# A third score slot, a buffer of its own for the attention output, eight gelu tiles in place of twelve, and new order lists

## The reference

```
x = x + attn(layernorm(x))     # 16 heads of 8; q = elu(q)+1, k = elu(k)+1
                               # weights = (rope(q) . rope(k)) / (q . k); out = weights @ v @ w_out + b_out
x = x + ffn(layernorm(x))      # router: softmax over 8 experts, the best 2, weights renormalized
                               # h = gelu(x @ W1[e] + b1[e]), y = h @ W2[e] + b2[e], all 8 experts;
                               # out = sum of y * combine + shared expert; F = 512
x = x + mamba(layernorm(x))    # in-projection, 4-tap conv, silu, dt = softplus(...)
                               # h = exp(dt*A)*h + dt*B*x, y = h . C, 16 states, 256 channels; norm, gate, out
x = x + ffn(layernorm(x))
```

## Time and profile before

| | us |
|---|---|
| median of 3 runs | 4017.41 (4011.95 to 4021.06) |
| the profiled execution | 4019.45 |
| its span | 4017.3 |
| PE busy | 3458.3 (86%) |
| ScalarE busy | 3227.9 (80%) |
| VectorE busy | 2936.5 (73%) |
| GpSimd busy | 1559.3 (39%) |
| DMA, mean share | 44.8% on the one hardware queue |

### The profile page before, as it was taken

How to read it: one execution, slowest core, us unless ns; L and a number is a source line. 1 busy time by engine, 2 the same in 40 slices (tenths; PEclk the granted TensorE clock), 3 DMA queues, 4 the chain that set the end, 5 groups by cost and what they waited for, 6 DMA issues and landing times.

```text
span 4017.3 us, 38974 instructions
## 1 busy us (share of the span) xinstructions
PE 3458.3 (86%) x11446; PEld 1464.2 (36%) x11446; DVE 2936.5 (73%) x3513; ACT 3227.9 (80%) x4037; POOL 1559.3 (39%) x758
## 2 busy tenths in 40 slices
PE   3786698989899898989989898989989898898847
PEld 1141233434333343433334343433334343344424
DVE  2427768788696868879696877869697886959592
ACT  3677688888888888988989888888988888886653
POOL 1112235435253544425253543524354442415261
PEclk9586799999999999999999999999999999998978
DMA  4142445544444545444544444545454444434432
GB/s 147 45 136 61 128 144 150 156 141 141 149 145 147 152 136 162 144 143 140 155 146 145 147 145 151 147 140 149 145 155 139 150 140 150 145 108 139 131 129 71
DMA packets 214852, 552.05 MB, mean 137 GB/s; under 512 B 25105, under 2 KB 96626, under 8 KB 214642
## 3 DMA queue, kind: packets, MB, share of 16 engines
q1 hardware_dynamic: 214642, 549.57, 44.8%
HBM read 488.65 MB, written 63.18 MB: 137 GB/s over the span
## 4 chain that ended last, share of the span: by engine, by line
PE 47%; DVE 19%; ACT 16%; issue 13%; POOL 4%; DMA 1%; SPq 1%; ACTq 0%; POOLq 0%; DVEq 0%
PE bank L782 15%; PE bank L734 5%; PE bank L771 5%; ACT rPool L884 4%; ACT L1022 4%; DVE ws L1220 4%; PE bank L712 4%; PE bank L673 4%; DVE rPool L1108 4%; PE bank L773 3%; PE bank L772 3%; PE bank L707 3%; DVE ws L1227 3%; ACT hF L884 3%; DVE ws L1216 2%
## 5 line engine op out<-in xcount | busy, mean ns | idle before, releaser
L782 PE MATMUL bank<-hF,wst 128*128 128x512 f32 x2304 | 1212.1, 643 | 68.3 <-DVE tmp L1178 62.6
L1108 DVE TENSOR_TENSOR rPool<-bank,rPool 128x512 f32<-128x512 f32 x1024 | 700.2, 684 | 461.1 <-PE bank L712 431.8
L884 ACT ACTIVATE hF<-bank,cols 128x512 f32<-128x512 f32 x1152 | 771.2, 687 | 249.7 <-PE bank L773 240.5
L1328 POOL TENSOR_TENSOR yM<-yM,ws 128x1024 f32<-128x1024 f32 x240 | 742.6, 3094 | 471.9 <-DVE ws L1227 461.1
L1313 POOL TENSOR_TENSOR acc<-acc,tmp 128x512 f32<-128x512 f32 x240 | 442.6, 1844 | 1123.1 <-DVE tmp L1178 1116.8
L884 ACT ACTIVATE rPool<-bank 128x512 f32<-128x512 f32 x1040 | 574.9, 594 | 271.2 <-PE bank L707 217.9
L1220 DVE TENSOR_TENSOR_SCAN ws<-dAs,ws 128x1024 f32<-128x1024 f32 x256 | 696.7, 2722 | 4.1 <-ACT dAs L884 1.5
L1022 ACT ACT_TABLE_LOAD x531 | 681.3, 1283 | 9.4
L771 PE MATMUL bank<-xnH,wst 128*128 128x512 f32 x1152 | 625.9, 543 | 73.0 <-ACT hF L884 69.8
L782 PEld LDWEIGHTS bank<-hF,wst 128*128 128x128 f32 x2304 | 426.1, 200 | 505.8 <-issue 368.9
L712 PE MATMUL bank<-qpk,kpk 48*128 48x512 bf16 x1024 | 421.4, 412 | 178.8 <-DVE rPool L1108 177.3
(11 more groups left out here) (154 smaller groups left out, 3031.9 us busy)
## 6 DMA issues: line engine op xcount, KB each, us to landing
wst<-wscr SPq DMA_DIRECT2D x288, 768.0 KB, 5.6
bc<-bcscr SPq DMA_DIRECT2D x256, 512.0 KB, 4.1
cB<-gscr SPq DMA_DIRECT2D x256, 256.0 KB, 4.7
qscr<-parts SPq DMA_DIRECT2D x192, 128.0 KB, 5.1
kscr<-parts SPq DMA_DIRECT2D x192, 128.0 KB, 2.1
kpk<-kscr SPq DMA_DIRECT2D x128, 192.0 KB, 5.9
qpk<-qscr SPq DMA_DIRECT2D x128, 192.0 KB, 6.4
wscr<-wst SPq DMA_DIRECT2D x9, 512.0 KB, 2.6
```

Of the source, the lines that this page charges most:

```text
L782: pe.matmul(ps[FFN][:, :], w2, hF[:, q % HSLOTS, :], start=(c == 0), stop=(c == FC - 1)).then_inc(s_dn, 1)
L884: return nc.scalar.activation(out_, in_, fn, **kw)
L1108: v.tensor_tensor(rP[:, step % 2, c, :], ps[NUM][:, :], rP[:, step % 2, c, :], ALU.mult).then_inc(s_mul, 1)
L1328: g.tensor_tensor(yM[:, :, :], yM[:, :, :], ws[:, s % 3, :, :], ALU.add).then_inc(s_ya, 1)
```

## The change

rPool grows from 8 units to 12, three slots of four, counted on from batch to batch (16 steps are not a multiple of three). The attention output has its own tile oT, and the eighth logarithm's wait goes. hF shrinks from 12 tiles to 8, also counted on over the feed-forwards (36 is no multiple of 8). Gelu waits for the down-projections only at even chunks, and then for one more than its own tile needs, so that it covers the next chunk as well. The lists of passes 2 to 16 (MAIN and LAST) are new on all five engines; those of pass 0, pass 1 and the end are not. Nothing is computed more or less, but for table loads: ScalarE's MAIN list has 34 for 33, its LAST list 50 for 41.

```diff
-HSLOTS = 12
+HSLOTS = 8
+RSLOTS = 3
...
     "ACT": """
-    T.gelu H.gelu*4 T.log A.ln N.decay A.ln*3 N.decay A.ex T.gelu H.gelu*2 F.mean H.gelu*2 T.log N.decay F.var
-    A.ln*3 T.gelu H.gelu*4 T.log A.ln*2 A.ex F.router T.gelu F.gelu*4 T.log A.ln*2 H.close A.ln N.decay P.load A.ex
+    T.gelu H.gelu*2 T.log A.ln*4 N.decay A.ex T.gelu H.gelu*2 F.mean H.gelu*6 T.log A.ln F.var N.decay A.ln*2
+    N.decay A.ln*2 T.gelu H.gelu*2 T.log A.ex A.ln F.router A.ln N.decay T.gelu F.gelu*4 T.log A.ln P.load H.close
...
-        rPool = sb("rPool", [P, 8, 512])
-        rP = rPool[:, :, :].rearrange("p (s c) t -> p s c t", s=2)
-        oT = rPool[:, 7, :]
+        rPool = sb("rPool", [P, RSLOTS * NC, 512])
+        rP = rPool[:, :, :].rearrange("p (s c) t -> p s c t", s=RSLOTS)
+        oT = sb("oT", [P, 512])[:, :]
...
-                                       rP[:, s % 2, c, :], start=(s == 0), stop=(s == STEPS - 1))
+                                       rP[:, (STEPS * b + s) % RSLOTS, c, :], start=(s == 0), stop=(s == STEPS - 1))
...
-                    pe.matmul(ps[FFN][:, :], w2, hF[:, q % HSLOTS, :], start=(c == 0), stop=(c == FC - 1)).then_inc(s_dn, 1)
+                    pe.matmul(ps[FFN][:, :], w2, hF[:, (NCH * f + q) % HSLOTS, :], start=(c == 0), stop=(c == FC - 1)).then_inc(s_dn, 1)
...
-                        act.wait_ge(s_av, floor(STEPS * b + s - 1))
-                    if n == 2 * NC - 1:
-                        act.wait_ge(s_oproj, floor(b))
+                        act.wait_ge(s_av, floor(STEPS * b + s - RSLOTS + 1))
                     act.wait_ge(s_den, floor(UNITS * b + n + 1))
-                    a(rP[:, s % 2, c, :], ps[n % 2][:, :], ACT.Ln).then_inc(s_ln, 1)
+                    a(rP[:, (STEPS * b + s) % RSLOTS, c, :], ps[n % 2][:, :], ACT.Ln).then_inc(s_ln, 1)
...
-                    act.wait_ge(s_dn, floor(NCH * f + n - HSLOTS + 1))
-                    a(hF[:, n % HSLOTS, :], ps[UP + n % 2][:, :], ACT.Gelu, bias=b1c[:, w * FC + c:w * FC + c + 1]).then_inc(s_ge, 1)
+                    if c % 2 == 0:
+                        act.wait_ge(s_dn, floor(NCH * f + n + 2 - HSLOTS))
+                    a(hF[:, (NCH * f + n) % HSLOTS, :], ps[UP + n % 2][:, :], ACT.Gelu, bias=b1c[:, w * FC + c:w * FC + c + 1]).then_inc(s_ge, 1)
```

More of the change, by code:

```diff
@@ L131 @@
+    G.w G.gate M.bc G.w*2 P.pk G.gate M.bc*2 P.pk G.gate P.ahead G.gate G.w P.ahead
 """,
     "PE": """
[L133 to L136 removed]
@@ L159 @@
+    T.gelu G.gelu M.row G.gelu T.log A.ln M.dt A.ln A.ex M.dt A.ln*2 M.sp T.gelu G.gelu*2 T.log M.decay A.ln*3 A.ex
+    A.ln M.decay A.ln*2 M.decay A.ex T.gelu G.gelu*2 P.cast G.gelu*4 T.log A.ln*4 M.decay A.ex M.decay T.gelu
+    G.gelu*2 P.cast G.gelu*2 T.log A.ln*4 A.ex A.ln*2 M.decay A.ln*2 A.ex M.decay T.gelu G.gelu*4 A.oT T.log
 """,
     "DVE": """
-    A.v H.part N.dbx F.mean A.mul N.scan A.mul N.hc H.part N.dbx A.mul N.scan A.mul N.hc H.part F.var N.dbx F.router
-    A.mul F.route H.part N.scan A.mul F.turn N.hc A.mul N.dbx A.mul P.mean N.scan A.mul N.hc F.part A.mul N.dbx
@@ L170 @@
+    F.part A.mul E.gate A.mul G.mean A.mul*3 F.part G.var G.router G.route F.part G.turn A.mul M.mean M.var M.conv*6
+    A.mul M.conv*2 A.mul G.part A.mul*6 M.dt M.dbx*2 M.scan M.hc A.mul G.part A.mul*2 M.scan A.mul M.hc A.mul M.dbx
+    A.mul M.scan M.hc A.mul*2 G.part M.dbx A.mul M.scan M.hc A.mul M.dbx A.mul G.part A.mul M.scan A.mul M.hc
+    A.mul*5 G.part A.mul*2 M.dbx*2 M.scan*2 M.hc*2 A.close
 """,
     "POOL": """
-    H.add*2 N.acc H.add N.acc H.add N.acc*3 F.add N.acc*2 P.rope P.rest F.add P.rest N.acc*2 P.rope P.rest F.add*4
@@ L173 @@
-    P.rest*2 F.add M.take P.rest*3 G.add*2 M.acc*3 G.add P.keep M.keep G.add M.acc*3
+    N.acc H.add N.acc H.add*3 N.acc*4 F.add P.rope N.acc*3 F.add*2 P.rope P.rest F.add P.rest*2 F.add P.rest F.add*2
+    M.take P.rest*2 M.keep G.add M.acc P.rest M.acc*2 P.rest M.acc G.add*3 P.keep M.acc*2
 """,
@@ L181 @@
+    G.w*2 M.bc G.gate M.bc G.gate*2 M.bc*2 G.w G.gate M.bc*3 G.out
 """,
     "PE": """
[L183 to L186 removed]
@@ L199 @@
+    M.row G.gelu M.dt G.gelu*2 M.dt T.log M.sp M.decay*2 T.gelu G.gelu*2 T.log M.decay T.gelu G.gelu*3 T.log
+    M.decay*2 T.gelu G.gelu T.silu M.silu T.log M.decay*2 T.gelu G.gelu*3 T.log M.decay T.gelu G.gelu*5 T.log
+    M.decay*2 T.gelu G.gelu*5 T.log M.decay T.gelu G.gelu T.log M.decay T.gelu G.gelu*2 T.log M.decay T.gelu
+    G.gelu*3 T.log M.decay T.silu M.silu T.gelu G.gelu*2 T.log M.decay T.gelu G.gelu T.log M.decay G.close
 """,
     "DVE": """
-    F.mean H.part N.dbx N.scan N.dbx N.scan H.part N.hc*2 F.var F.router H.part N.dbx F.route N.dbx H.part N.scan
@@ L207 @@
-    M.scan G.part M.hc M.dbx M.scan M.hc M.dbx M.scan M.hc
+    F.mean N.dbx H.part N.scan N.hc N.dbx H.part N.scan N.dbx N.hc H.part F.var F.router N.dbx H.part N.scan F.route
+    N.hc N.scan F.turn N.hc N.dbx F.part N.scan N.dbx N.hc N.scan F.part N.hc N.dbx N.scan N.hc F.part N.dbx N.scan
+    F.part N.dbx N.hc N.scan F.part N.hc E.mean F.part E.var F.part E.gate G.mean G.var F.part G.router G.route
+    F.part G.turn M.mean M.var M.conv*8 G.part*2 M.dt M.dbx M.scan M.hc M.dbx M.scan M.hc M.dbx M.scan M.hc M.dbx
@@ L212 @@
+    G.add M.acc G.add M.acc G.add*2 M.acc*2 M.keep
 """,
```

110 lines of the change are left out of this document (49 added, 61 removed).

## The result

Of two sets of runs on one chip each, the changed kernel's has a median of 3867.68 us (3862.55 to 3874.12, 4 runs) and the old one's 4017.75 us (4 runs). The ratio is 0.9629, with a 95% interval of 0.9608 to 0.9649: 150 us are gone where 34 were forecast, and the time lies 67 us under the low end of the range. The profiled execution has a span of 3869.4 us.

What follows compares the result with a forecast made beforehand. It took ScalarE as pacing, with fixed order on three mutually waiting queues holding the passes. Per pass 1.28-2.2-0.9-0.5 = -2.3, times 14 is -32.5, less 2 for pass 1 and 2.04, from 4019.45: 3983 us, range 3935 to 4055.

Steps and rivals of the forecast that it cites:

- head of the pass: Turn of a middle pass around VectorE's xFin write: PE's stop goes, router read earlier; -2.2 us per pass, bounds -1.0 and -3.8.
- the sum: All terms added: -2.3 us per middle pass, times 14 is -32.5, with -2 for pass 1; 3983 us.
- third slot: Score buffer in middle passes, used in 4 steps of 16: -0.9 us per pass, bounds 0 and -1.75.
- slower rival: PE waits for a later xFin at the mean, slow clock behind it: +2.1 us per pass, 4052 us; chance 0.34.
- ScalarE as the pacing engine: Middle passes: ScalarE taken to set the pace, so nothing covers one more table load at the pass end; +1.28 us per pass.
- +1.28 per pass: Price of one additional ScalarE table load at the end of each middle pass, with nothing covering it.
- first rival: PE waits for a later xFin if six scan instructions take their mean or more: 4052 us; chance 0.34.
- Gelu pairs: ScalarE's gelus beyond the first two of a burst fall from 20 pairs to 19: -0.5 us per pass, bounds 0 and -0.5.
- The last pass: Nine more ScalarE table loads, 11.5 us, in the last pass: taken as 0, bounds 0 and +11.5.
- Passes 0 and 1: Lists kept: pass 0 unchanged at 196.8 us though ScalarE's 27.8 us of slot waits go; pass 1 -2, bounds 0 and -5.7.

Runs made afterwards that it cites:

- 512-column run: Changed kernel plus one unneeded GpSimd addition on 512 columns per accumulation, beside VectorE's scan: 4013.16 us, ratio 0.9979 to the kernel before.
- the four moved groups: Changed kernel with two score slots, attention-value groups of steps 1, 2, 3 and 7 moved ahead in PE's main list: 4064.74 us, ratio 1.0109.
- Two places: Changed kernel with GpSimd's x copy and additions, and VectorE's scan and two multiplications behind xFin, put back as before: 3896.82 us together; alone 3904.56 and 3887.05.

## Why the prediction was wrong

The step that failed is the choice of **durations**: the term for VectorE's work was priced as if the new order left the instructions' lengths alone. I priced them by their means before, or their shortest, only in the head of the pass, and let every other one keep its length. I named longer scans as a sign against me and never costed the opposite, though the earlier trace rows held both ends: a multiplication of 1.22 us against a mean of 1.676, 240 of them, a scan of 2.28 in the trace against 2.722, 256 of them. Taken to the shortest, these two groups alone hold 240 x 0.46 + 256 x 0.44 = 223 us. The change took 61.2 and 93.0 of it, 154 us (696.7 less 635.5, 401.0 less 308.0). The overlap given back by the 512-column run costs 145 us, so this is what the sum lacked; it is had only together with the third slot, which the sum had at -0.9 per pass. I cited the rule of the two engines only inside the slower rival.

Point by point:
- *ScalarE as the pacing engine.* Not borne out: its 32 us of loads were worth about 8, and 32 lies outside what the noise allows. So the +1.28 per pass should have been smaller, some +0.3. And ScalarE's busy time did not even rise by it: 200.94 us in the middle pass where it was 200.77, since its longer bursts made up for the load. ScalarE is the busiest by real durations (84%); PE's waits for VectorE go better with the time (the table above).
- *The head of the pass.* The mechanism came out as told. With T the end of the last score product (2415.12), PE starts the mean at T+10.9 without a wait (forecast T+11.0), xFin is done at T+9.6 (T+10.2 to 12.5), the centring starts at T+12.0 (13.3 to 14.8) and the scaling at T+27.8 (27.6 to 29.1), PE's stop at the down-projection is gone, and so are the lower clock behind it (1.00 in the window shown) and ScalarE's 3.76 us. The six scan instructions took 9.1 us, even less than my shortest price of 9.4, because GpSimd stood still in front of xFin. Too small was the gain at the end: the router's result is read at T+31.3 and not T+34.7 to 36.2, of which 3.0 us are the two casts that I had left at their old lengths. The head gained 5.9 us against T+37.2, where I took 2.2.
- *The first rival* (the wait moves to xFin) fell with that: its condition, a GpSimd backlog beside the six, was the one thing that the new order removed.
- *The third slot.* -0.9 per pass was wrong as a method. I counted in how many steps it is used and shared the waits out evenly. Under the new lists it is worth 197/14 = 14 us a pass (with the four moved groups), and the buffers alone under the old lists 23/14 = 1.6. The worth of a slot depends on the order around it.
- *Gelu pairs.* -0.5 forecast; ScalarE's wait for up-projections rose from 20.3 to 23.5 over two passes, +1.6 a pass. The 8 tiles can't be told apart from that by these runs.
- *The last pass.* I took 0 with +11.5 as a bound; it gained 24 in the profiled runs, of which the last pass's lists alone bring 17 (368.6 less 351.7).
- *Passes 0 and 1.* Pass 0 was right: 196.8 and 198.3, ScalarE's slot wait of 27.8 turned into another (its wait for the score matmuls went from 18.6 to 42.4), VectorE's 55.4 for numerators is 56.8. Pass 1's -2 came out as +3.9, and both are below what a profiled run can tell.
- *The sum.* The forecast's terms, with all their low or all their high bounds added, give 3945 to 4033 and not the 3955 to 4008 that the prediction states; the measured time lies outside either. -2.3 a pass forecast, -9.7 measured. The head accounts for up to 3.7 of the missing 7.4, and the rest goes, as far as the runs tell, with the other scans and multiplications of the pass: VectorE is busy 13.6 us less in it (180.90 and 167.29).

What stays open: which of the other moves in the main lists bring the accumulations away from the scans. Two places together are worth 25 to 30 us of the 116. Open, too, is what the fall of PE's waits for ScalarE (159.1 to 70.5) is worth: the 512-column run leaves them low and still loses the gain, and with GpSimd's additions short the old lists have 156.0 and the new 90.1 at a distance of 30 us, but no run changes ScalarE's main list alone. The granted clock over the run went from 0.931 to 0.943, and what that gives back is in every figure here and apart in none.

## What to carry to other kernels

Before a reordering is costed, look for instructions of one form that have two lengths in the trace, and at what ran beside the long ones; if it is the same neighbour each time, the order itself has a price or a gain, and its bound is the count times the spread. Do not judge such an edit by the mean of one kind of instruction, since a meeting that is avoided in one place often turns up at the next; look at the engine's whole busy time, and above all at who waits for it, since the place of a long instruction counts as much as its length. A microsecond of VectorE's was worth 0.35 to 0.83 in the edits of the new kernel, and in the old one a kernel with 21 us more of it was 25 us faster. And a buffer is judged together with the order that uses it: one slot was worth 23 us under one set of lists and up to 197 under the other.
